# Moving five pieces of work within one step of an attention and expert kernel

## The reference

```python
q = split_heads(_proj(x, Wq, bq))        # x is the normalized input
k = split_heads(_proj(c, Wk, bk))
v = split_heads(_proj(c, Wv, bv))
q = _apply_rotary(q_emb, q)
k = _apply_rotary(k_emb, k)
scores = jnp.einsum('bhtc,bhsc->bhts', q, k) / math.sqrt(K_CH)
p_attn = jax.nn.softmax(scores, axis=-1)
out = jnp.einsum('bhts,bhsc->bhtc', p_attn, v)
out = out.transpose(0, 1, 3, 2).reshape(b, N_HEADS * K_CH, t_t)
return _proj(out, Wo, bo)
```

## Time and profile before

| | us |
|---|---|
| median of 3 runs | 761.05 (760.6 to 761.88) |
| the profiled execution | 760.41 |
| its span | 758.6 |
| TensorE busy | 697.3 (92%) |
| VectorE busy | 598.5 (79%) |
| ScalarE busy | 512.7 (68%) |
| GpSimd busy | 426.0 (56%) |

### The profile page before, as it was taken

One profiled execution on the slowest core, in us unless ns is written; L12 is line 12 of the kernel. 1 busy time (PEld: TensorE's weight loads), 2 busy tenths in 40 slices (PEclk: granted clock), 3 DMA queues, 4 the chain that ended last, 5 costly groups with the idle time before them and its releaser, 6 DMA issues.

```text
span 758.6 us, 19342 instructions
## 1 busy us (share of the span) xinstructions
PE 697.3 (92%) x5941; PEld 482.6 (64%) x5941; DVE 598.5 (79%) x1597; ACT 512.7 (68%) x1211; POOL 426.0 (56%) x755
## 2 busy tenths in 40 slices
PE   2698999999999999999999999999897999999995
PEld 1355565666666666666666666666565978888784
DVE  6888999899899889989998998998645544466666
ACT  4267787888888888888888888887751155554441
POOL 3554656645756667666666566664344025655562
PEclk9999999999999999999999999999999999999998
DMA  5665543444465455544444444444073535678774
GB/s 170 175 174 161 156 124 107 124 134 145 141 176 156 150 164 147 155 131 138 142 143 152 146 121 149 137 140 153 32 225 116 165 92 162 221 244 279 230 236 151
DMA packets 97147, 118.81 MB, mean 157 GB/s; under 512 B 12821, under 2 KB 81304, under 8 KB 97049
## 3 DMA queue, kind: packets, MB, share of 16 engines
q1 hardware_dynamic: 89684, 100.16, 44.0%
q0 software_dynamic: 6864, 16.93, 6.4%
q10 hardware_dynamic: 500, 0.49, 0.3%
HBM read 76.87 MB, written 42.11 MB: 157 GB/s over the span
## 4 chain that ended last, share of the span: by engine, by line
PE 69%; DVE 12%; POOL 8%; issue 7%; DMA 2%; ACT 1%; another core or an unknown queue 0%; SPq 0%; ACTq 0%; DVEq 0%; POOLq 0%
PE bank_o L1376 13%; PE bank_s L1402 11%; PE bank_st L1439 10%; PE bank_st L1559 9%; DVE M L1157 5%; PE bank_s L1577 4%; PE bank_st L1354 4%; PE bank_b L1420 2%; POOL work L739 2%; POOL parts_sb L742 2%; POOL work L744 2%; PE bank_b L1446 2%; PE bank_a L1494 2%; PE bank_b L1485 2%; PE bank_s L1361 2%
## 5 line engine op out<-in xcount | busy, mean ns | idle before, releaser
L1157 DVE TENSOR_REDUCE M<-bank_s 128x2 f32<-128x512 f32 x512 | 339.3, 682 | 49.4 <-PE bank_s L1402 41.5
L826 ACT ACTIVATE Pr<-bank_st 128x512 f32<-128x512 f32 x503 | 292.6, 598 | 64.0 <-PE bank_st L1439 53.3
L1402 PE MATMUL bank_s<-QK 72*128 72x256 bf16 x1024 | 202.0, 280 | 8.8 <-DMA QK<-parts 5.9
L1439 PE MATMUL bank_st<-QK 98*128 98x256 bf16 x1006 | 195.8, 276 | 0.9 <-ACT Pr L826 0.2
L1376 PE MATMUL bank_o<-Pr,wide 128*32 128x256 f32 x2048 | 140.3, 390 | 0.5 <-ACT Pr L826 0.5
L1402 PEld LDWEIGHTS bank_s<-QK 72*128 72x128 bf16 x1024 | 91.0, 99 | 68.8 <-DVE M L1157 30.6
L739 POOL TENSOR_TENSOR work<-work 128x256 f32<-128x256 f32 x62 | 45.0, 725 | 158.5 <-DVE work L1215 158.5
L766 POOL DMA_INDIRECT results<-Pr,ids_out x79 | 78.5, 994 | 80.4 <-issue 45.7
L1439 PEld LDWEIGHTS bank_st<-QK 98*128 98x128 bf16 x1006 | 90.4, 98 | 45.9 <-ACT Pr L826 18.7
L1559 PE MATMUL bank_st<-QK,xn 128*128 x316 | 82.3, 383 | 1.0 <-issue 1.0
L1376 PEld LDWEIGHTS bank_o<-Pr,wide 128*32 128x32 f32 x2048 | 56.3, 110 | 36.0 <-issue 15.0
(11 more groups left out here) (175 smaller groups left out, 1061.2 us busy)
## 6 DMA issues: line engine op xcount, KB each, us to landing
QK<-parts SPq DMA_DIRECT2D x127, 288.0 KB
parts<-parts_sb SPq DMA_DIRECT2D x64, 192.0 KB, 2.4
wide<-slots SPq DMA_DIRECT2D x79, 130.0 KB
ctx_kv<-ctx_dram SPq DMA_DIRECT2D x64, 128.0 KB, 2.4
xT_all<-results SPq DMA_DIRECT2D x14, 512.0 KB
QK<-w_gu SPq DMA_DIRECT2D x8, 512.0 KB
parts<-parts_sb SPq DMA_DIRECT2D x31, 128.0 KB, 2.9
X<-x_dram SPq DMA_DIRECT2D x7, 512.0 KB, 5.4
```

Source lines behind the costliest of these rows:

```text
L826: nc.scalar.activation(Pr[k][:], bank_of_scores(at.r, k)[:], ACT.Exp, scale=SCALE).then_inc(s_exp, 1)
L1157: nc.vector.tensor_reduce(M[:, c, 2 * ORDER[k]:2 * ORDER[k] + 2], bank_s[S_BANK[c][k]][:].rearrange("p (a s) -> p a s", a=2), AX.X, ALU.ma ...
L1402: last = nc.tensor.matmul(bank_s[S_BANK[at.mod(2)][k]][:, T * t:T * t + T], Q[c][0:KR, ORDER[k], P * t:P * t + P], K[c][0:KR, ORDER[k], :] ...
L1439: last = nc.tensor.matmul(bank_of_scores(at.r, k)[:, T * s:T * s + T], K[c][0:MROW + 2, ORDER[k], P * s:P * s + P], Q[c][0:MROW + 2, ORDER ...
```

## The change

On each engine the same work stands in another order; nothing is added or taken away.

- TensorE: the projection goes from k=4 (behind score 4) to k=3 in front of score 3, that is right behind the first value burst. The output transposes go from k=6 (in front of score 7) to k=7 behind transposed score 7. The row transposes go from k=7 of the odd step to k=0 of the even step, behind transposed score 0.
- ScalarE: the first swap goes from k=4 to k=3, the second stays at k=5.
- VectorE: the logit add goes from behind maximum 2 to behind maximum 1 (in step 64 it stays at k=3).
- GpSimd: the maxima split goes in front of L744, the second of two subtractions that follow L742.

```diff
-        SWAP_APART = 1
+        SWAP_APART = 2
@@ gpsimd
-                    wait(pool, s_p1, at.value(1, 7))
-                    nc.gpsimd.tensor_tensor(rest[:, h], qk[:, h], parts[:, p, h, 0, :], ALU.subtract).then_inc(s_r1, 1)
                 if at.has(2) and at.r != -2:
                     split_maxima(at)
                 if at.has(6) and at.r >= -4:
 
                     p, h = at.odd_pair(6), at.mod(2)
+                    wait(pool, s_p1, at.value(1, 7))
+                    nc.gpsimd.tensor_tensor(rest[:, h], qk[:, h], parts[:, p, h, 0, :], ALU.subtract).then_inc(s_r1, 1)
@@ scalar
-                        if k == 4 + SWAP_APART * half and at.has(6):
+                        if k == 3 + SWAP_APART * half and at.has(6):
@@ vector
-                    if k == (3 if at.r == DRAIN else 2) and at.r % 2 == 0 and at.has(-6):
+                    if k == (3 if at.r == DRAIN else 1) and at.r % 2 == 0 and at.has(-6):
@@ tensor
-                    if k == 4 and at.has(6):
+                    if k == 3 and at.has(6):
...
+                    if even and k == 0 and at.has(-6):
+
+                        wait(pe, s_xs, at.pairs(-6, add=1))
+                        held(at, bank_b, (s_rope, at.value(1, 6), NB))
...
-                    if even and k == 6 and at.has(-2):
+                    if even and k == 7 and at.has(-2):
...
-                    if not even and k == 7 and at.has(-5):
-
-                        wait(pe, s_xs, at.pairs(-5, add=1))
-                        held(at, bank_b, (s_rope, at.value(1, 7), NB))
```

More of the change, by code:

```diff
@@ L1393, in step @@
                 for k in range(H):
-                    if at.has(2):
-                        c = at.mod(4, 2)
-                        if k == 0:
-                            v = 32 * ((at.r + 2) // 4 + 1)
-                            wait(pe, s_stk[c], v if at.i is None else 32 * at.i + v)
-                        wait(pe, s_red, at.value(8, 16 + k + 1 - S_BACK[at.mod(2)][k]))
-                        for t in range(2):
-                            last = nc.tensor.matmul(bank_s[S_BANK[at.mod(2)][k]][:, T * t:T * t + T],
-                                                    Q[c][0:KR, ORDER[k], P * t:P * t + P], K[c][0:KR, ORDER[k], :],
-                                                    start=True, stop=True)
-                        last.then_inc(s_S, 1)
-                    if k == 4 and at.has(6):
+                    if k == 3 and at.has(6):
                         p = at.odd_pair(6)
@@ L1426, in step @@
                                              start=True, stop=True).then_inc(s_bias, 1)
+                    if at.has(2):
+                        c = at.mod(4, 2)
+                        if k == 0:
+                            v = 32 * ((at.r + 2) // 4 + 1)
+                            wait(pe, s_stk[c], v if at.i is None else 32 * at.i + v)
+                        wait(pe, s_red, at.value(8, 16 + k + 1 - S_BACK[at.mod(2)][k]))
+                        for t in range(2):
+                            last = nc.tensor.matmul(bank_s[S_BANK[at.mod(2)][k]][:, T * t:T * t + T],
+                                                    Q[c][0:KR, ORDER[k], P * t:P * t + P], K[c][0:KR, ORDER[k], :],
+                                                    start=True, stop=True)
+                        last.then_inc(s_S, 1)
                     if at.has(0):
@@ L1442, in step @@
                         last.then_inc(s_ST, 1)
+                    if even and k == 0 and at.has(-6):
+                        wait(pe, s_xs, at.pairs(-6, add=1))
+                        held(at, bank_b, (s_rope, at.value(1, 6), NB))
+                        for c in range(2):
+                            last = nc.tensor.transpose(bank_b[:, P * c:P * c + P],
+                                                       ring[:, at.pair(-6) % RING, P * c:P * c + P], ident[:])
+                        last.then_inc(s_xt, 1)
                     if not even and k == 1 and at.has(-3):
@@ L1496, in step @@
                         last.then_inc(s_vp, 1)
-                    if not even and k == 7 and at.has(-5):
-                        wait(pe, s_xs, at.pairs(-5, add=1))
-                        held(at, bank_b, (s_rope, at.value(1, 7), NB))
-                        if at.i is None:
-                            wait(pe, s_x2, at.pairs(-3, add=1), NP)
-                        for c in range(2):
-                            last = nc.tensor.transpose(bank_b[:, P * c:P * c + P],
-                                                       ring[:, at.pair(-5) % RING, P * c:P * c + P], ident[:])
-                        last.then_inc(s_xt, 1)
                     g = PLACED.index((at.r, k)) if (at.r, k) in PLACED else -1
```

## The result

The changed kernel takes 774.38 us, the median of four runs (773.05 to 776.32), where the kernel before took 761.0 beside it. The ratio is 1.0176, with an interval of 1.0151 to 1.0202: slower, and above the range of the prediction. The profiled execution took 773.59 us with a span of 771.5, 12.9 us more than before.

A forecast was written before the change was run, and what follows sets the result against it. TensorE and VectorE were both taken as near full, bound by waits for each other. Attention +0.6, early steps +0.8 and end 0 summed to +1.4 us on 760.41: 761.8 us, 762.4 on the median of runs; range 757 to 767.

The forecast's parts named there:

- The bound and the circle: Score 3: VectorE idles 0.9 us in front of maximum 3; the odd projection waits about 0.6 us for the residual add.
- signs: Timeline marks of the forecast: waits at transpose, scores 1 or 2, odd projection and maximum 3; two steps 16.0 to 16.1 us.
- Leg A: From score 3 of an odd step to score 3 of the next even step: 7.98 us before, 7.88 to 8.17 forecast.
- Leg B: From score 3 of an even step to score 3 of the next odd step: 8.06 us before, 7.74 to 8.44 forecast.
- The early steps: Steps before 12, with more VectorE statistics: +0.15 us in each of five pairs, +0.8 us in sum.
- The end: From step 58 on, no projection left and nobody waiting for what moves: 0, bounds -0.5 and +1 us.
- The one that the projection is paid for in full: Slower rival: residual add ends 0.25 us later still, +6 us, 767 to 768 us; chance 0.38 together with its +2 to +4 form.
- point of decision: The slower rival decides where leg B's maximum 5 starts later than 1.65 us behind score 3.
- smaller form: Slower rival's milder form: each wait for the residual add 0.1 us longer than worked out, +2 to +4 us.
- likeliest case: Whole kernel about the same, 762.4 us on the median, own range 759.5 to 765.3; chance of same 0.36.
- The faster rival: Routing operations on VectorE get clear of GpSimd at the shared ports: 756 to 757 us, chance 0.26.

The follow-up runs named there:

- the last (near 281 us): Changed kernel with the odd projection back behind score 4 and SyncE's wait in front of the maxima's transfer removed; ratio 0.9839 to the kernel before.
- the first session: Four edits run beside the kernel before (748.7 us): projection not moved 0.9791, residual add sooner 1.0031, split not moved 1.0343, projection alone 1.0404.

## Why the prediction was wrong

**The bound and the circle: right.** The prediction said that VectorE would idle for score 3 where the projection stands in front of it, and that the odd projection would wait for the residual add. Both are there, with 1.10 us of idle time (0.9 forecast) and 0.60 us of wait in step 31 (0.6 forecast), 0.59 in step 29, 0.48 in step 33, and none in step 35, the one without routing operations. Two more of its signs came: no wait for GpSimd in front of the maxima transpose, and a wait for a maximum in front of scores 1 or 2 of even steps (0.28 us in step 30, just short of the 0.3 that it named). One did not: two steps take 16.46 us and not 16.0 to 16.1.

**Leg A: right to 0.07 us.** By kind of odd step (19, 21, 23, 17 and so on) it is 7.92, 8.20, 7.89 and 8.20 where 7.88, 8.17, 7.88 and 7.98 were forecast; the mean is 8.05 against 7.98. Only the last is off, and not by the logit add, to which the forecast had given 0.1 us: in step 34 that ends 0.19 us before the projection starts. Instead the product of the logits waits for ScalarE's copy of the row transposes, and takes 0.60 us where it takes 0.45 in step 32:

```profile
325.89 0.52 PEld L1461 LDWEIGHTS bank_b<-wr,xT_all 128*128 128x128 f32 x4 [0.18 <-ACT xT_all L881]
```

**Leg B: the step that failed.** 8.57, 8.60, 8.47 and 7.97 us where 8.10, 8.44, 8.08 and 7.74 were forecast, in sum 1.25 us more in eight steps. With the 0.3 us of leg A that makes 1.55, and over the 5.5 groups of the 44 steps 8.5 us of the 9.3 that the steps became longer; the forecast had 0.6 for the whole stretch. So the mechanism was right and the sizes of terms in leg B were not. Taken apart on the step to 31: the rotary pair ends 3.59 us behind score 3 (3.61 forecast), the output transposes start at 3.69 (3.71), score 0 at 4.55 (4.41), the residual add ends at 8.01 (7.92), the projection starts at 8.11 (8.00) and score 3 at 8.61 (8.44). Three terms were too small:

- The routing operations behind maxima 0 and 1 of odd steps. I took their sizes from the rows of before, in which L744 stands earlier. With L749 now beside them L1037 lasts 0.57 instead of 0.23 us and L1050 0.64 instead of 0.18; L1041, in step 31 beside L750, lasts 0.55 instead of 0.42. That is 0.34 and 0.46 us in front of the residual add in two of four kinds of steps and 0.13 in a third. The first two are shown by the kernel with the split back, which gets 0.35 and 0.42 us back in just these two kinds. L1041 is as long there, so its 0.13 us come from something else; with the transposes alone it also reaches 0.56 us. The prediction had weighed the ports as a way to be faster, with the argument that the operations stand where they stood, relative to the rotary pair. They do (L1037 of step 31 stands 1.41 us behind the end of the rotary pair in both traces); it is GpSimd's long operation that was moved against them. That was to be read in GpSimd's order, and I read it for the split alone.
- The projection itself: 0.51 us (odd steps) and 0.53 us (even steps) from its start to score 3's, where 0.44 stood in the earlier trace rows. It was priced between scores; behind the value burst it takes this much, whether it has waited or not.
- The output transposes with the value projection: 299.44 - 298.58 = 0.86 us where I had 0.25 and 0.45. The two float32 pieces now stand one behind the other, and the value projection then takes 0.52 us in every kernel with this order; the other 0.09 us are the transposes' (0.34), which take 0.23 us in this place in the kernel without the projection's move.

The second term is 0.07 to 0.09 us in every leg. The third is 0.16 us, but where the projection waits for the residual add it is covered; it shows in steps like 35 alone (7.97 against 7.74).

**The early steps: 3.1 us, forecast 0.8.** 1.1 us of them are there at step 3, from the filling of the pipeline, for which the forecast had nothing. At step 1 it is even 2.4 us; between the two the trace of before has a stretch of half clock, at 58.2 us, which that of the changed kernel has not. The five pairs from step 3 to 13 lose 2.0 us. From steps 7 and 9 on a pair takes 16.94 us against 16.71 and 16.73, near the forecast. One pair, from step 5 to 7, takes 17.91 against 16.85. Step 6 holds the constants of the routing on VectorE, and the logit add, now behind maximum 1, stands behind them with the projection waiting for it (VectorE's timeline, then TensorE's):

```profile
94.70 0.58 DVE L1017 COPY CU<-small 1x16 f32<-1x16 f32 x1
95.20 0.16 DVE L1182 TENSOR_TENSOR LG<-bank_b,br 128x16 f32<-128x16 f32 x1
```

```profile
95.46 0.67 PE L1408 MATMUL bank_b<-xn,w_qk 128*128 128x256 f32 x2 [0.93 <-issue]
```

Of a move that a loop makes in every step, the one step with other work in it has to be looked at on its own.

**The end: 0.5 us, forecast 0 with a bound of 1.** It is the sum of two things that the forecast did not have: steps 57 to 61 take 29.3 us where they took 30.5, and what follows takes 1.7 us more. In this sparse part the changed kernel has 6.8 us at a granted clock of 0.50:

```profile
586.40:593.20 6.80, 4.50 (x20) 4.21 (x20) 3.77 (x19) 0.56 (x2) 0.48 (x1) 0.50 0.07 25
```

Up to 630 us it has two more of 3.4 us, at 562.5 and 624.0; the trace of before has one of 3.4 us, at 549.7. That fits the 1.7 us, but no run here separates it from the order of work, so it is argued and not shown.

**The rivals.** None of them reached 774 us. The one that the projection is paid for in full gave 767 to 768. Its point of decision, maximum 5 later than 1.65 us, did not come true (the rotary pair ended on time); the queue behind the rotary pair did it. Its smaller form named the right wait, "0.1 us longer than I worked out", but leg B came out 0.16 to 0.47 us longer. That slower had the highest chance, 0.38, rests in part on the reason that did not hold, so as far as that goes the direction was luck. The likeliest case's own range was made from 0.1 us of error in each pair of steps. The terms of a chain can all be off in one direction, as here, and the sum counts them 28 times: the real error was 0.4 us in a pair. The faster rival had the mechanism of the ports right and its sign wrong.

**The two gains that were hidden.** The split and the transposes were worth 8.9 us in the 44 steps by themselves, and the prediction did not sum them without the projection. A sum without it would have shown how much the projection's move may cost, 8.9 us in the 44 steps, before the change is a loss.

## What to carry to other kernels

Before an operation is moved in front of the work that another engine waits for, look for the circle: if its own wait is for something in that engine's queue, everything in that queue is paid for on both engines, here 14.4 us for one 0.5 us projection in every second step. Durations of small VectorE operations with two inputs in SBUF hold only for the GpSimd operation that stood beside them: when GpSimd's order is changed, place its long operations anew against VectorE's rows before a duration of before is used. And a change of several parts is best summed part by part: here two parts gave 2.1%, and the third took 3.9% away.

## What the runs showed of the hardware

- A VectorE operation of 128x64 with two SBUF operands took 0.21 to 0.23 us beside small GpSimd operations and up to 0.57 us beside one of 0.67 us (the changed kernel, the kernel with the split back); one of 128x16 took 0.16 to 0.64 us. Started under L749, they ended 0.04 and 0.08 us behind it.
- In the kernel without the projection's move L1037 takes up to 0.58 us too, and that kernel is 2.1% faster than before: there nobody waits long for the residual add behind it.
- A float32 projection of 128x256 takes 0.43 to 0.44 us of TensorE between scores in the kernel before, and 0.51 or 0.53 us right behind the value burst in the changed one.
- Stretches of 3.4 us at half clock fell into the attention of the kernel with the split back five times (near 116, 218, 287, 372 and 440 us), with TensorE busy 6.30 of the 7 us in front of one of them. From 172 to 480 us no other kernel has one, except the last (near 281 us); in front of 172 us some have one or two. The cause stays open.
- The kernel before takes 748.7, 759.7 and 761.35 us in three sessions. From score 3 of step 61 to the end the kernels of the first session take 211 to 213 us, and all others 222 to 228, before and changed among them, while the changed kernel's 44 steps are 362.3 and 362.2 us in two sessions. Most of that difference lies in front of the experts' first tile (L1254), which starts 67 to 68 us behind score 3 of step 61 in the first session and 76 to 81 us behind it in the others. The traces of the first session have no half clock there and the others 3.4 to 13.6 us of it, which is too little for the whole difference; what makes it is not known.
